# Between gathers: an add that nobody reads in place of a wait for a landing

## The chip, the core and the metric

One NeuronCore of one Trainium2 chip runs the kernel. The metric is the device time of one execution in microseconds. TensorE, VectorE, ScalarE, GpSimd and SyncE each run a list of instructions in order and meet through semaphores.

## The reference, cut to what matters

A graph layer over 3125 nodes with 256 features: `xn` is the layer norm of `x`, and

```
x = x + gnn(xn, src, dst, edge_weight) + mix(xn)      # mix: linear attention, then a small MLP
x = x + ffn(layernorm(x))                             # ffn: two of eight experts, chosen by a router

msgs = edge_val[:, None] * X[edge_col]                # gnn, 53125 edges
h = segment_sum(msgs, edge_row, num_segments=3125)
return h @ W.T + b
```

The kernel computes `X @ W.T` first (the tensor `xg_rows` in DRAM) and sums the weighted rows of it afterwards. The change is in the fetching of those rows.

## The kernel before, in words

**The columns.** The edges are sorted on the chip by destination tile of 128 nodes into 440 columns of 128 edges (`COLS`). For each column GpSimd issues one indirect DMA (`gather`, L705) that fetches the 128 source rows of 256 f32 from `xg_rows` into one of the 18 slots of `RING`, a part of the tile `ARENA`. VectorE makes a 128x128 selection matrix for it (`select`, L1277). TensorE multiplies the two (L1799), two columns at a time: a pair. VectorE adds each product to its tile of `X` (`add`, L1289). Six columns are a hand, and TensorE waits at the start of a hand until all its six gathers have landed. Three hands are a round of the ring. A gather into a slot that was used before waits until TensorE has finished the pair that read it (`chunk_mm`).

**Order of the work.** The first 132 columns (`COLS_A`) are worked off while the edges of the later groups are still being sorted; there GpSimd has a multiply (`group_columns`, L693) after every sixth gather. From column 132 on GpSimd only gathers; the first of these 308 gathers starts at 318.06 us and the last at 786.42. Beside these 308 columns the attention and the MLP run. In part A (12 steps, `a_transpose`, `a_project` L1850 and L1857, `a_outer` L1865) keys, values and queries are projected, and VectorE adds KS (L1338) and QT (L1341). In part B (12 full steps of seven pairs, `b_attend` L1895, `b_transpose` L1636, `b_hidden` L1913, `b_project` L1924) the attention output goes through VectorE and ScalarE (which writes XS, L900) and back to TensorE. The pairs are woven by hand between the steps: `pairs(p, p + 2)`, a piece of the step, and so on, and VectorE's `columns` in the same way. Every engine keeps this order, so what waits in it holds back all behind it.

**The wait that the change touches.** `BREATH` is 8. Before columns 132, 140, ... 436 (39 times) GpSimd waits until the gather issued last has landed: `landed(c - 1)` gives the semaphore of its hand and the count it then has.

**After the gathers** come the residuals, and the expert FFN from about 800 us on. SyncE loads the eight experts' first weights, 512 KB each, during the gathers, one for every nine pairs of even number (L591).

`Chain` counts the marks of one engine on one semaphore: `mark` adds one when the instruction is done, `settle` waits until all marks so far are in.

Of the kernel before, what the change touches and what calls it, by code (L numbers as in the profile page):

```python
# [5 lines left out]
def gps_layer_program(nc, x, row, col, weight, gnn_wT, gnn_b, qkv_wT, ln1_g, ln1_b, mix_w1T, mix_b1,  # L6
# [10 lines left out]
    ALU, ACT, AX = mybir.AluOpType, mybir.ActivationFunctionType, mybir.AxisListType  # L17

    P = 128
    N, C = out.shape  # L20
# [22 lines left out]
    HAND = 6  # L43
    HANDS = 3
    RC = HANDS * HAND
# [25 lines left out]
    with ctx:  # L71
        def sb(name, shape, dt=f32):
            return scope.enter_context(nc.sbuf_tensor(name, shape, dt))

        def sem(name):
            return ctx.enter_context(nc.semaphore(name))
# [11 lines left out]
        ROWC = sb("ROWC", [P, 5, C])  # L88
        B2R, L2G, L2B, FG, FB = (ROWC[:, n, :] for n in range(5))
        carrier = sb("carrier", [P, 1])  # L90
        eps_ln = sb("eps_ln", [P, 1])
        warm = sb("warm", [P, 1])
        ident = sb("ident", [P, P])
# [232 lines left out]
        gathered = [sem(f"gathered{h}") for h in range(HANDS)]  # L326
# [184 lines left out]
        def pair_bank(pair):  # L511
            return bank[(2 if pair < PAIRS_A else 6) + pair % 2]

        def landed(c):

            r, at = divmod(c, RC)
            return gathered[at // HAND], 16 * (r * HAND + at % HAND + 1)

        def per_chunk(m, G, n):

            return m[:, G * GC:(G + 1) * GC].rearrange("p (k o) -> p k o", o=1).to_broadcast([P, GC, n])
# [91 lines left out]
        def _(pool):  # L613
            chain = Chain(pool, pool_step)
# [83 lines left out]
            def gather(c):  # L698

                r, at = divmod(c, RC)  # L700
                k = at % HAND
                if r and k % 2 == 0:
                    pair = (c - RC) // 2
                    pool.wait_ge(chunk_mm[pair % 2], pair // 2 + 1)
                pool.indirect_dma_start(RING[:, at, :], None, xg_dram,  # L705
                                        bass.IndirectOffsetOnAxis(ap=SIX[:, c:c + 1], axis=0)
                                        ).then_inc(gathered[at // HAND], 16)
# [17 lines left out]
            pool.wait_ge(slots_ready, 2)  # L725
            for c in range(COLS_A, COLS):
                if (c - COLS_A) % BREATH == 0:
                    pool.wait_ge(*landed(c - 1))
                gather(c)


# [272 lines left out]
        def _(dve):  # L1004
# [260 lines left out]
            def targets(r, cols=RC):  # L1265

                _, base = nc.values_load_multi_w_load_instructions(
                    BID[0:1, bass.ds(r, 1), 0:cols].rearrange("p a c -> p (a c)"), engines=[mybir.EngineType.DVE],
                    min_val=0, max_val=(TILES - 1) * C,
                    skip_runtime_bounds_check_because="BID counts the buckets whose first column is at or before the "  # L1270
                    "column, less one: the first bucket starts at column 0, so it lies in 0 .. TILES - 1, times C")
                return base
# [235 lines left out]
            def over_sum(dst, width, n):  # L1508
# [14 lines left out]
            dve.wait_ge(topi_ready, 1)  # L1523
            dve.wait_ge(up_in, 16 * (NE + 1))
            _, chosen = nc.values_load_multi_w_load_instructions(
                RI[0:1, 0:TOPK], engines=[mybir.EngineType.DVE], min_val=0, max_val=NE - 1,
                skip_runtime_bounds_check_because="RI holds places of the NE experts that max_index found")
# [586 lines left out]
```

## Time and profile before

| | |
|---|---|
| median of 3 runs | 972.7 us (970.0 to 973.05) |
| the profiled execution | 975.65 us |
| its span | 973.9 us |
| TensorE busy (matmul) | 785.4 us, 81% |
| VectorE busy | 677.2 us, 70% |
| GpSimd busy | 584.6 us, 60% |
| ScalarE busy | 415.0 us, 43% |
| gathers, GpSimd's part | 440, 426.6 us, mean 0.97 us |

The span runs from the first to the last instruction; the execution's own time has 1.75 us around it. Busy time is the time inside instructions. "Idle before" is how long the engine had stood still when an instruction began, and the releaser is what ended it, as inferred from semaphores; "issue" means that the profile shows no releaser. The busy time of a gather is the time in which GpSimd writes its transfer list; the transfer itself goes on after it.

### The profile page before, as it was taken

What the parts mean: (1) busy time and instruction counts of PE and PEld (TensorE: products, weight loads), DVE (VectorE), ACT (ScalarE), POOL (GpSimd) and SP (SyncE); (2) the same over time, 40 slices, a digit from 0 to 9 for tenths busy, and PEclk for the clock granted to TensorE, in tenths of its full rate; (3) what the DMA queues carried; (4) which work ended last, traced back from release to release, by engine and by line L of the source; (5) the groups of instructions that cost most, each with busy time, mean ns of one, the idle gap of its engine ahead of it and who ended that gap; (6) DMA issues with size and microseconds to landing.
All of it is one profiled execution on the core that took longest, in us unless ns stands there. A gap on an engine that the chain in (4) does not pass through costs nothing.

```text
span 973.9 us, 14063 instructions
## 1 busy us (share of the span) xinstructions
PE 785.4 (81%) x4353; PEld 639.0 (66%) x4353; DVE 677.2 (70%) x1936; ACT 415.0 (43%) x1008; POOL 584.6 (60%) x648
## 2 busy tenths in 40 slices
PE   7879857887787888878777877777776677999997
PEld 5649846776676566546545655565555454999997
DVE  8989737999875546445545767677667567766776
ACT  2738724775772133313313222332223216666551
POOL 3847675878877666666666666666666610333353
PEclk9989977999989799999988988989989889999999
DMA  7210032333233433333233333333332521000000
GB/s 238 87 49 1 28 92 60 93 88 88 87 91 92 111 87 103 87 87 108 82 105 90 114 87 84 106 91 108 90 111 87 100 30 55 13 22 24 23 29 30
DMA packets 38994, 76.88 MB, mean 79 GB/s; under 512 B 9811, under 2 KB 22536, under 8 KB 38920
## 3 DMA queue, kind: packets, MB, share of 16 engines
q0 software_dynamic: 21120, 57.70, 21.5%
q1 hardware_dynamic: 17800, 18.29, 5.9%
q8 instruction: 35, 0.57, 0.2%
q14 instruction: 39, 0.32, 0.1%
HBM read 69.48 MB, written 6.48 MB: 78 GB/s over the span
## 4 chain that ended last, share of the span: by engine, by line
PE 33%; issue 14%; POOL 11%; DVE 9%; ACT 4%; another core or an unknown queue 2%; DMA 1%; DVEq 1%; POOLq 0%; ACTq 0%
PE bank L2008 14%; POOL ARENA L705 11%; PE bank L1799 7%; DVE X L1289 4%; PE bank L1850 4%; ACT OIA L824 2%; PE bank L1857 2%; PE bank L1865 1%; PE bank L1636 1%; PE bank L1757 1%; PE bank L1913 1%; DMA ARENA<-xg_rows,ARENA 1%; DVE ARENA L1277 1%; DVE ST L1029 1%
## 5 line engine op out<-in xcount | busy, mean ns | idle before, releaser
L705 POOL DMA_INDIRECT ARENA<-xg_rows,ARENA x440 | 426.6, 970 | 214.5 <-issue 118.0
L1289 DVE TENSOR_TENSOR X<-bank,X 128x256 f32 x440 | 185.0, 420 | 217.0 <-PE bank L1799 91.2
L1799 PE MATMUL bank<-ARENA 128*128 128x256 f32 x880 | 246.7, 421 | 97.1 <-DVE X L1289 53.2
L1799 PEld LDWEIGHTS bank<-ARENA 128*128 128x128 f32 x880 | 173.1, 208 | 148.4 <-DVE X L1289 67.0
L1277 DVE TENSOR_SCALAR ARENA<-iota,ARENA 128x128 f32<-128x128 f32 x440 | 153.4, 354 | 0.0
L1757 PE MATMUL bank<-OIA,ASA 128*128 128x128 f32 x676 | 95.3, 308 | 14.8 <-DVE ASA L1207 5.8
L1757 PEld LDWEIGHTS bank<-OIA,ASA 128*128 128x128 f32 x676 | 93.7, 224 | 18.5 <-issue 17.4
L824 ACT ACTIVATE OIA<-iota,LANE 128x128 f32<-128x128 f32 x286 | 86.0, 388 | 13.9 <-PE bank L1757 13.6
L992 ACT ACTIVATE HF<-bank,FB 128x262 f32<-128x262 f32 (+1 forms) x96 | 46.8, 488 | 42.0 <-PE bank L2008 22.5
L868 ACT ACTIVATE NK<-bank 128x256 f32<-128x256 f32 x25 | 9.7, 388 | 123.0 <-PE bank L1850 101.7
L2008 PE MATMUL bank<-QH,W1L 128*128 128x262 f32 (+1 forms) x192 | 55.9, 291 | 2.3 <-DVE W1L L1535 1.7
L2008 PE MATMUL bank<-QH,W1H 128*128 128x262 f32 (+1 forms) x192 | 55.2, 287 | 0.0
L2008 PE MATMUL bank<-QL,W1H 128*128 128x262 f32 (+1 forms) x192 | 55.1, 287 | 0.0
L693 POOL TENSOR_TENSOR ASA<-LHA,EPC 128x832 f32<-128x832 f32 x26 | 41.3, 1590 | 22.6 <-DVE LHA L1192 20.8
L2008 PE MATMUL bank<-W2H,HFL 128*128 128x256 f32 x192 | 54.0, 281 | 0.0
L2008 PE MATMUL bank<-W2H,HFH 128*128 128x256 f32 x192 | 54.0, 281 | 0.0
L2008 PE MATMUL bank<-W2L,HFH 128*128 128x256 f32 x192 | 53.9, 281 | 0.0
L1850 PE MATMUL bank<-QKVW,XT 128*128 128x512 f32 x100 | 49.3, 639 | 0.0
L734 POOL TENSOR_TENSOR XN<-XN,B2C 128x256 f32<-128x256 f32 x25 | 18.8, 752 | 47.7 <-DVE B2C L1566 47.7
L992 ACT ACTIVATE HFH<-bank,FB 128x262 fp32r<-128x262 f32 (+1 forms) x96 | 47.0, 490 | 0.0
L833 ACT COPY GSW<-bank 64x128 f32<-64x128 f32 x32 | 8.3, 258 | 82.7 <-remote 32.4
L1574 DVE TENSOR_TENSOR HFL<-HF,HFH 128x262 fp32r<-128x262 f32 (+1 forms) x96 | 40.1, 467 | 4.2 <-ACT HFH L992 3.9
(317 smaller groups left out, 1532.6 us busy)
## 6 DMA issues: line engine op xcount, KB each, us to landing
ARENA<-xg_rows,ARENA POOLq DMA_INDIRECT x440
FW1A<-in_exp_w SPq DMA_DIRECT2D x8, 512.0 KB
xg_rows<-XGS SPq DMA_DIRECT2D x12, 256.0 KB, 2.1
out<-YO SPq DMA_DIRECT2D x24, 128.0 KB, 1.7
X<-in_x SPq DMA_DIRECT2D x1, 1664.0 KB, 12.7
X<-in_x SPq DMA_DIRECT2D x1, 1536.0 KB, 8.3
FW<-in_exp_w SPq DMA_DIRECT2D x2, 512.0 KB, 4.4
QKVW<-in_qkv_wT SPq DMA_DIRECT2D x1, 768.0 KB
```

Of the source, the lines that this page charges most:

```text
L693: made = pool.tensor_tensor(into[:, :, LC:2 * LC], lh, per_chunk(EPC, G, LC), ALU.mult)
L705: pool.indirect_dma_start(RING[:, at, :], None, xg_dram, bass.IndirectOffsetOnAxis(ap=SIX[:, c:c + 1], axis=0)).then_inc(gathered[at // HA ...
L824: ins = act.activation(into[:, k, :], iota[:, :], ACT.Abs, scale=-1.0, bias=LANE[:, G * GC + k:G * GC + k + 1])
L992: ins = act.activation(into, bank[s][:, 0:width], ACT.Gelu, bias=FB1[:, n // FJ, n % FJ:n % FJ + 1])
L1277: ins = V.tensor_scalar(SEL[:, t % 2 * HAND + k, :], iota[:, :], SLO[:, at], SW[:, at], ALU.is_equal, ALU.mult)
L1289: V.tensor_tensor(xt, pair_bank(pair)[:, half * C:(half + 1) * C], xt, ALU.add).then_inc(x_added, 1)
L1574: V.tensor_tensor(HFL[par][:, n, 0:width], HF[:, s, 0:width], HFH[par][:, n, 0:width].bitcast(f32), ALU.subtract).then_inc(hl_ready, 1)
L1757: ins = T.matmul(bank[s][:, 0:P], left[:, k, :], right[:, k, :], start=(k == 0), stop=(k == GC - 1))
L1799: ins = T.matmul(pair_bank(pair)[:, u * C:(u + 1) * C], SEL[:, t % 2 * HAND + k, :], RING[:, h * HAND + k, :], start=True, stop=True)
L1850: ins = T.matmul(bank[2 + s][:, :], XT[:, c, s, :], QKVW[:, c, C:3 * C], start=(c == 0), stop=(c == CC - 1))
L1857: ins = T.matmul(bank[5][:, h * 2 * P:h * 2 * P + n], QKVW[:, c, h * P:(h + 1) * P], XT[:, c, 0:len(slots), :], start=(c == 0), stop=(c == ...
L2008: ins = T.matmul(into, left, right, start=(m == 0), stop=(m == len(terms) - 1))
```

## The change

In place of the wait for a landing, GpSimd waits for its own last mark (`settle`) and adds the rows L2G and FG (128x256 each) into `rest`, a new tile that nothing reads. The count of gathers, their order, the ring and every other wait stay. `landed` goes, since nothing calls it.

```diff
         carrier = sb("carrier", [P, 1])
+        rest = sb("rest", [P, C])
...
-        def landed(c):
-
-            r, at = divmod(c, RC)
-            return gathered[at // HAND], 16 * (r * HAND + at % HAND + 1)
...
             for c in range(COLS_A, COLS):
                 if (c - COLS_A) % BREATH == 0:
-                    pool.wait_ge(*landed(c - 1))
+                    chain.settle()
+                    chain.mark(pool.tensor_tensor(rest[:, :], L2G, FG, ALU.add))
                 gather(c)
```

## Rows read from the trace of the kernel before

**Rows 1.** The page: shares of the chain of work that ended last, by engine.

```profile
PE 33%; issue 14%; POOL 11%; DVE 9%; ACT 4%; another core or an unknown queue 2%; DMA 1%; DVEq 1%; POOLq 0%; ACTq 0%
```

**Rows 2.** Waits of TensorE, 330 to 570 us: total us, times, longest.

```profile
PE bank L1799 <- issue: 12.8, 6, 4.2
...
PE bank L1799 <- DMA ARENA<-xg_rows,ARENA: 0.5, 1, 0.5
```

**Rows 3.** The same, 570 to 790 us.

```profile
PE bank L1799 <- issue: 20.7, 11, 5.3
...
PE bank L1799 <- DMA ARENA<-xg_rows,ARENA: 3.5, 2, 2.2
```

**Rows 4.** Timeline, GpSimd and TensorE: start, us, instruction, idle before.

```profile
689.90 0.95 POOL L705 DMA_INDIRECT ARENA<-xg_rows,ARENA  x1 [0.30 <-issue]
...
692.72 1.10 PE L1799 MATMUL bank<-ARENA 128*128 128x256 f32 x4 [3.43 <-issue]
```

**Rows 5.** Timeline of GpSimd around a multiply between gathers.

```profile
210.13 0.95 POOL L705 DMA_INDIRECT ARENA<-xg_rows,ARENA  x1 [0.30 <-issue]
211.10 1.59 POOL L693 TENSOR_TENSOR ASA<-LHA,EPC 128x832 f32<-128x832 f32 x1
212.85 0.99 POOL L705 DMA_INDIRECT ARENA<-xg_rows,ARENA  x1 [0.16 <-PE bank L1799]
```

**Rows 6.** Timeline of GpSimd: gathers before and behind waits for a landing.

```profile
329.82 0.95 POOL L705 DMA_INDIRECT ARENA<-xg_rows,ARENA  x1 [2.04 <-DMA ARENA<-xg_rows,ARENA]
...
338.60 0.95 POOL L705 DMA_INDIRECT ARENA<-xg_rows,ARENA  x1 [0.30 <-issue]
341.62 0.95 POOL L705 DMA_INDIRECT ARENA<-xg_rows,ARENA  x1 [2.07 <-DMA ARENA<-xg_rows,ARENA]
...
514.90 0.94 POOL L705 DMA_INDIRECT ARENA<-xg_rows,ARENA  x1 [2.13 <-DMA ARENA<-xg_rows,ARENA]
...
766.59 0.95 POOL L705 DMA_INDIRECT ARENA<-xg_rows,ARENA  x1 [2.12 <-PE bank L1799]
```

**Rows 7.** The chain in order of time: start, us; L1850 in A, L1913 in B.

```profile
335.54 3.85 PE bank L1850 x8
...
375.51 3.43 PE bank L1850 x8
...
388.14 3.43 PE bank L1850 x8
...
510.53 1.73 PE bank L1850 x4
...
528.73 3.78 PE bank L1913 x8
...
755.67 1.73 PE bank L1913 x8
```

**Rows 8.** Waits of TensorE, 534 to 650 us, first half of B.

```profile
PE bank L1636 <- ACT XS L900: 11.1, 4, 3.8
...
PE bank L1799 <- issue: 1.5, 1, 1.5
```

**Rows 9.** Timeline of TensorE and GpSimd near the last gathers.

```profile
776.07 2.05 PE L1799 MATMUL bank<-ARENA 128*128 128x256 f32 x4 [5.34 <-issue]
...
787.61 6.67 PE L1799 MATMUL bank<-ARENA 128*128 128x256 f32 x16 [3.91 <-issue]
...
782.49 0.94 POOL L705 DMA_INDIRECT ARENA<-xg_rows,ARENA  x1 [6.20 <-DMA ARENA<-xg_rows,ARENA]
```

**Rows 10.** Groups of GpSimd: busy us, mean ns, idle before.

```profile
L735 POOL TENSOR_TENSOR X<-X,ROWC 128x256 f32<-128x256 f32 x25 | 21.3, 851 | 0.0
L734 POOL TENSOR_TENSOR XN<-XN,B2C 128x256 f32<-128x256 f32 x25 | 18.8, 752 | 47.7 <-DVE B2C L1566 47.7
```

**Rows 11.** Timeline: a gather beside VectorE's QT addition.

```profile
384.80 1.82 POOL L705 DMA_INDIRECT ARENA<-xg_rows,ARENA  x1 [0.30 <-issue]
...
385.11 0.69 DVE L1341 TENSOR_TENSOR QT<-QR,EQ 128x512 f32<-128x512 f32 x1
```

## The prediction

> **What bounds the kernel now.** I first read the chain of work that ended last [rows 1]. TensorE's own work is a third of it, GpSimd 11%, and "issue" 14%, which is time in which an engine stood still and the profile names no releaser. The change touches only the last 308 of the 440 gathers (columns 132 to 439), which run from about 318 to 787 us, so the question is what TensorE stands still for there. The waits of TensorE over that stretch say it [rows 2, 3]: its pair matmuls (L1799) were idle before 12.8 us by "issue" and 0.5 by a named gather in 330 to 570 us, and 20.7 and 3.5 in 570 to 790 us. One case in the timeline shows what "issue" is [rows 4]: the sixth gather of a hand starts at 689.90 and ends at 690.85, and the pair that needs it starts at 692.72, 1.87 us after, having idled 3.43 us. So a gather lands some 1.9 us after GpSimd has finished it, and TensorE stood waiting for that landing. The four entries add up to 37.5 us. That is the most that quicker gathers can give while TensorE's other waits stay as they are.
>
> Then GpSimd itself. Inside a run of gathers one starts every 1.25 us (0.95 of work, 0.30 of gap). Every eighth time the wait for the landing makes the gap 2.07 us instead of 0.30: the gather at 338.60 and the next at 341.62 [rows 6]. Eight gathers and a breath took (514.90 - 329.82) / 15 = 12.34 us in the attention's first part and (766.59 - 514.90) / 21 = 11.99 us after it [rows 6], so 1.54 and 1.50 us a column.
>
> **The change, part by part.**
>
> *The wait that goes.* There are 39 of them (132, 140, ... 436). Each costs 2.07 - 0.30 = 1.77 us of GpSimd's time.
>
> *The add that comes.* 39 adds of 128x256 f32, two inputs in SBUF. This very form stands in the trace: 25 at a mean of 0.75 us (L734) and 25 at 0.85 (L735) [rows 10]. What an add costs between gathers is seen where GpSimd multiplies between two of them [rows 5]: the multiply of 1.59 us starts as soon as the gather ends, and the gathers on either side start at 210.13 and 212.85, 2.72 us apart where 1.25 is usual. So the insertion costs 1.47 us, its own 1.59 less 0.12, and the gather behind it is 0.04 longer. For an add of 0.75 to 0.85 this is 0.67 to 0.77; between gathers I take 0.68, since the 0.85 comes from a stretch where VectorE too works on SBUF operands most of the time. The settle in front of it asks for the add of eight gathers before, which is long done, so it costs nothing; what hides the add's own completion is 10 us of gathers, and without that cover it would cost at most the add's length again.
>
> *Net on GpSimd.* 1.77 - 0.68 = 1.09 us a time, 42.5 us in all. A breath then takes 12.34 - 1.09 = 11.25 us in the first part, 1.41 a column, and 10.90 later, 1.36 a column.
>
> *What TensorE makes of it, first part (A).* A step of the attention's first half holds on average 4.83 pairs, 9.67 columns (by the source, pairs 66 to 123 over 12 steps). By the chain, twelve steps took 510.53 - 335.54 = 175.0 us, 14.58 each; a step in which TensorE had columns enough took 388.14 - 375.51 = 12.63 [rows 7]. The new gather rate allows 9.67 x 1.41 = 13.6 us a step, and GpSimd, which starts A with a lead, may spend it. I take 13.5: 12 x 1.1 = 13 us. Bounds: 6 us if the waits on VectorE's KS and sums take half of it back, 19 us if steps of 13.0 are reached.
>
> *Second part (B).* Eleven steps of 7 pairs, 14 columns, took (755.67 - 528.73) / 11 = 20.63 us [rows 7]. The new gather rate allows 14 x 1.36 = 19.1, which would be 17 us. But here I doubt it. In 534 to 650 us TensorE hardly waited for gathers (1.5 us), and was no quicker; it stood 11.1 us for ScalarE's XS in the transposes [rows 8]. These waits are those of B's own loop (attend, VectorE's sums, ScalarE's scaling, transpose), and where gathers are late they hide behind them. So B may give nothing (its own loop is as slow as the gathers) or 17. I take 8, half way, as the rows show both kinds of step.
>
> *The end.* At 770 to 788 us gathers land very late once: GpSimd waits 6.20 us for one, and TensorE 5.34 and 3.91 us [rows 9]. A GpSimd that is not halted after every eighth gather runs ahead until the ring of 18 stops it, so it would have several columns in hand there. I take 6 of the 9.25 us; bounds 0 and 9.25.
>
> *VectorE.* The add reads SBUF, as do VectorE's KS and QT additions. Beside QT (385.11, 0.69 us) a gather took 1.82 us instead of 0.95 [rows 11]: the two do get in each other's way. The Trainium skill (SBUF — State Buffer, Who interferes with whom) says that a VectorE instruction with two SBUF inputs and a GpSimd instruction that reads SBUF exclude each other for a whole instruction, whoever starts first. It speaks against the change: if each add blocked VectorE once for its length it would be 39 x 0.75 = 29 us of VectorE. The common VectorE instruction here, L1289, has one input in PSUM, and by the source the two-input ones are five or so in a step. If one add in ten meets one it is 4 x 0.75 = 3 us, most of it beside VectorE's own idle time; I put it at nothing and leave 3 us for the range. Nothing else is moved: SyncE's weight loads hang on the pair counter and come earlier with it.
>
> Sum: 13 + 8 + 6 = 27 us. The profiled execution took 975.65 us (span 973.9 and 1.75 around it), so 948.6. The median of the runs is 2.95 lower; if the late landings at the end belong to this execution alone, the gain is smaller and the start lower as well. By the median it would be 945.7; I say 947.
>
> **The rivals.**
>
> 1. *TensorE's and VectorE's own loops are the bound nearly throughout* (gain 6 to 15 us, 960 to 970). For it: B's first half, where no gather was waited for and the steps were as long [rows 7, 8]. Against it: A's quick steps of 12.63 and the 37.5 us of waits for landings. Worked out: A's lower bound 6, B 0, the end 0, is 970; with A's 13 it is 963.
>
> 2. *All of the waiting for gathers goes* (37.5 us, 938). For it: the new rate in B, 19.1 us a step, is well below what the steps take, and lateness at the start of a hand spreads to VectorE. Against it: XS waits.
>
> 3. *Slower: the halt kept the gathers in a good state.* Without it more transfers may be in flight, and landings like that at 782 us (6.20 instead of 2.07) become common. One such episode costs TensorE 5.34 + 3.91 = 9.25 us [rows 9]. Against 27 us gained, three more cancel the gain; from the fourth on the kernel is slower, with six 975.65 - 27 + 55 = 1004. Against it: halting every eighth time did not prevent that one, and the gathers before 318 us run without any such wait, six and a multiply in 5 x 1.25 + 2.72 = 9.0 us (1.5 a column, the mean rate of the later ones too), at 0.95 each [rows 5]. What the trace cannot show is more than the 14 in a row that the source issues at its start.
>
> 4. *The swap does nothing*: an add between gathers costs as much as the halt, 1.77 us, because engine changes are dear. [Rows 5] exclude it nearly: no gap before the multiply, 0.16 behind it.
>
> **How the numbers follow.** Forecast, 940 to 960: 0.52. Rival 2 (below 940): 0.12. Rival 1 (960 to 970): 0.20. Rivals 4 and a total absorption, within 0.3% (2.9 us, about what a measurement of this kernel can tell from no change): 0.08. Rival 3: 0.08. Range 935 to 969: it leaves out some 2 in 10, and takes in the bounds (13 + 8 + 6 becomes 6 + 0 + 0 or, capped, 37.5, and 3 us more for the slightly quicker matmuls of an engine that stands less, as the eight of L1850 took 3.85 us in one step and 3.43 in another [rows 7]). Faster 0.84, same 0.08, slower 0.08.
>
> **What would show it right or wrong.** In the changed kernel's timeline of GpSimd: after every eighth gather an add of 0.75 us with no gap, then 0.16, and no "DMA" releaser; from gather 132 on some gaps released by TensorE's pairs, the sign that the ring is full. The last gather should start 30 us or more earlier than 786.42. TensorE's waits on "issue" and gathers at L1799 should fall from 37.5 us to under 15, A's steps to 13.5, B's to 19.9. If B's steps stay at 20.6 with the XS waits grown, rival 1 holds. If gathers take longer than 0.95 us in bulk, or landings longer than 1.9, rival 3. I would be wrong above all if the lead of the gathers is eaten by VectorE, which is busy 70% of the span and works its column sums in order with everything else.

## The result: slower, and what the profile after shows

The changed kernel takes 981.2 us (median of 7 runs, 977.0 to 986.0), the kernel before 973.1 on the same chip (7 runs, 970.0 to 976.4). The ratio is 1.0092, with a 95% interval of 1.0062 to 1.0121. It is slower by 0.9%, where 2.7% faster was forecast. The profiled execution took 977.0 us (span 975.3), the quickest of its runs; that of before took 975.65, one of the slower of its. So the two traces show why the gain of 27 us is not there, and only 1.4 of the 8 us of loss.

**GpSimd did what was forecast around the adds.** Its timeline around a new add, then its waits from 318 to 800 us (total us, times, longest). They answer to [rows 5, 6]:

```profile
338.58 0.95 POOL L701 DMA_INDIRECT ARENA<-xg_rows,ARENA  x1 [0.30 <-issue]
339.54 0.74 POOL L725 TENSOR_TENSOR rest<-ROWC 128x256 f32<-128x256 f32 x1
340.44 0.97 POOL L701 DMA_INDIRECT ARENA<-xg_rows,ARENA  x1 [0.16 <-issue]
```

```profile
POOL ARENA L701 <- issue: 79.6, 277, 0.3
POOL ARENA L701 <- remote: 29.0, 19, 3.0
POOL ARENA L701 <- PE bank L1796: 23.9, 12, 5.8
```

The add follows the gather at once, the next gather 0.16 us behind it, and no DMA releases anything. Apart from one wait of 3.4 us at the first add, GpSimd halts only where the ring is full: 12 times on a pair of TensorE and 19 times on "remote". So the last gather starts only 6.6 us earlier, at 779.83 instead of 786.42, where 30 us or more were forecast: the ring gave most of the lead back.

**TensorE no longer waits for gathers.** Its waits before pairs, 318 to 800 us:

```profile
PE bank L1796 <- DVE X L1286: 31.4, 21, 4.4
...
PE bank L1796 <- issue: 2.3, 4, 1.2
```

The 37.5 us of [rows 2, 3] (37.7 over this whole stretch) have become 2.3, and no gather is named.

**Something else grew.** In the chain of work that ended last, GpSimd's 11% of [rows 1] are gone. VectorE has doubled, and "another core or an unknown queue" went from 2 to 7%:

```profile
PE 31%; DVE 18%; issue 11%; another core or an unknown queue 7%; ACT 3%; DVEq 1%; POOLq 0%; POOL 0%; ACTq 0%
```

There is no other core here. The label means that a semaphore rose at a time at which no recorded instruction ended. In the lists of waits the same thing is called "remote". VectorE's waits before its column adds, 318 to 800 us, first before the change, then after:

```profile
DVE X L1289 <- PE bank L1799: 80.4, 40, 6.9
DVE X L1289 <- issue: 56.8, 28, 7.0
DVE X L1289 <- remote: 37.5, 20, 4.3
```

```profile
DVE X L1286 <- remote: 73.5, 27, 8.3
DVE X L1286 <- PE bank L1796: 62.8, 33, 7.4
DVE X L1286 <- issue: 25.3, 22, 4.8
```

One episode shows what is behind it. The timelines of the changed kernel's engines, 338 to 355 us:

```profile
342.99 1.10 PE L1796 MATMUL bank<-ARENA 128*128 128x256 f32 x4 [1.56 <-DVE X L1286]
354.25 2.13 PE L1862 MATMUL bank<-VX,KS 128*128 128x132 f32 x8 [10.16 <-DVE KS L1335]
...
350.51 0.42 DVE L1286 TENSOR_TENSOR X<-bank,X 128x256 f32 x1 [7.41 <-remote]
...
353.09 1.11 DVE L1335 TENSOR_TENSOR KS<-KR,EXK 128x512 f32<-128x512 f32 x1
...
345.98 0.38 ACT L865 ACTIVATE NK<-bank 128x256 f32<-128x256 f32 x1 [11.36 <-remote]
...
346.72 0.95 POOL L701 DMA_INDIRECT ARENA<-xg_rows,ARENA  x1 [0.30 <-issue]
350.65 0.94 POOL L701 DMA_INDIRECT ARENA<-xg_rows,ARENA  x1 [2.98 <-remote]
```

TensorE's last pair is recorded from 342.99 to 344.09, and its projections (L1847) as ended by 338.40. ScalarE, which reads them, could go on at 345.98 and 350.20. VectorE, which reads the pairs, stood for 7.41 us until 350.51, and TensorE then stood for 10.16 us for VectorE's KS. Even GpSimd, whose ring was full, stood 2.98 us. The trace also holds the times at which semaphores rose. I set each rise of a TensorE semaphore beside the recorded end of the matmul that raises it:

```
semaphore of        matmul ended   semaphore rose
a pair   (L1796)    333.82         336.76
a pair   (L1796)    334.96         341.71
project  (L1847)    336.68         345.96
project  (L1847)    338.40         350.18
         (L1854)    340.12         350.27
         (L1633)    340.56         350.33
a pair   (L1796)    341.43         350.39
a pair   (L1796)    344.09         350.45
```

The last five come 0.06 to 0.09 us apart, up to 11.8 us after their work. The burst comes 3.5 us after the last gather started, when GpSimd had stood idle since 347.67. I call this a held update. The ends of matmuls are modelled, so "late" has some slack, but the starts are recorded and the next matmuls had begun. The engines that read the results did start only behind the late rises. Whether the rise alone is late, or the writing of the result before it, the trace does not tell.

I then counted the held updates, in 318 to 790 us: rises over 1 us after the end of the instruction that causes them, among those for which the trace has both.

```
          TensorE: late / recorded, sum    VectorE late    ScalarE late
before    55 / 230, 125 us                 0 of 366        0 of 90
after     77 / 221, 262 us                 0 of 372        0 of 92
```

Before had them too. In 800 to 974 us, where GpSimd gathers nothing, none of some 150 is over 0.3 us late in either kernel. The first 113 us, ahead of the first gather, show the same: none of 95 before and of 92 after is late. Between 113 and 318 us, where the first 132 gathers run with a multiply after every sixth, 37 to 45 of some 105 are late in every kernel of this document (before 44 of 102, 137 us in all; after 41 of 110, 120 us).

By the starts of TensorE's pairs, 66 to 124, to 208, to 219: the first part (A) went from 176.7 to 181.5 us, the second (B) from 248.6 to 255.6, the end from 35.6 to 25.0. That is 4.8 + 7.0 - 10.6 = 1.2 us, near the difference of the two profiled spans (1.4). The first step of A alone, with the episode above, went from 14.95 to 24.42 us.

**The two parts lost their time in different ways.** The same stretches, with the busy time of PE, PEld, DVE, ACT and POOL, the granted clock, the DMA share and GB/s; first A and B before the change, then A and B after:

```profile
331.92:508.65 176.73, 145.01 (x568) 99.63 (x568) 87.32 (x259) 54.65 (x134) 115.91 (x116) 0.94 0.33 95
508.65:757.23 248.58, 186.98 (x820) 144.49 (x819) 173.92 (x645) 72.86 (x123) 157.78 (x166) 0.92 0.33 96
```

```profile
331.75:513.27 181.52, 141.89 (x568) 100.21 (x567) 89.65 (x260) 55.18 (x134) 133.06 (x137) 0.92 0.33 97
513.27:768.80 255.53, 198.34 (x820) 153.87 (x819) 180.94 (x648) 72.87 (x123) 177.22 (x191) 0.87 0.33 95
```

In A, TensorE stands longer, 39.6 us instead of 31.7. The waits for gathers fell from 13.3 to 1.9 us, but those for KS rose from 9.4 to 18.4 and those of pairs for VectorE's adds from 2.9 to 11.3. VectorE's "remote" in this stretch rose from 8.6 to 44.6 us: all of its growth is here. In B, "remote" did not grow (28.9 us before, 26.1 after), and TensorE stands 4.4 us *less*, 57.2 instead of 61.6. There the same 820 matmuls are busy for 198.3 us instead of 187.0, with a granted clock of 0.87 instead of 0.92: it was at 1.2 GHz, the lower of its two levels, for 68 of 256 us where it had been for 41 of 249. This is not of the profiled execution alone: the seven runs of the change were granted 0.901 to 0.917 over the whole of them (mean 0.910), the kernel before 0.921 in the mean of its 64 runs beside the experiments, on four chips. In the episode above the clock was at 1.2 GHz from 344.5 to 358.2 us, through TensorE's stand and 4 us beyond it. Whether the held updates are what lowers it in B no run isolates; the last table has it for every kernel.

### The profile page after: what moved, and what is told of

Its sections match the earlier page's. It is cut to its first block, busy times and chain, and to the rows that moved or that the text cites. A ratio compares the mean times of both kernels' runs of the same rounds, so it can differ in the third digit from the quotient of the medians.

```text
span 975.3 us, 14064 instructions
## 1 busy us (share of the span) xinstructions
PE 792.4 (81%) x4353; PEld 646.4 (66%) x4353; DVE 682.0 (70%) x1936; ACT 415.3 (43%) x1008; POOL 613.5 (63%) x687
## 4 chain that ended last, share of the span: by engine, by line
PE 31%; DVE 18%; issue 11%; another core or an unknown queue 7%; ACT 3%; DVEq 1%; POOLq 0%; POOL 0%; ACTq 0%
PE bank L2005 14%; DVE X L1286 8%; PE bank L1796 6%; PE bank L1847 2%; DVE ARENA L1274 2%; PE bank L1633 1%; PE bank L1862 1%; PE bank L1754 1%; PE bank L1854 1%; PE bank L1921 1%; DVE ST L1026 1%; DVE KS L1335 1%; DVEq L1264 1%; DVE TX L1380 1%
## 5 line engine op out<-in xcount | busy, mean ns | idle before, releaser
L1796 PE MATMUL bank<-ARENA 128*128 128x256 f32 x880 | 242.8, 417 | 65.5 <-DVE X L1286 61.4
L1274 DVE TENSOR_SCALAR ARENA<-iota,ARENA 128x128 f32<-128x128 f32 x440 | 157.9, 364 | 0.0
L889 ACT ACTIVATE SD<-MV,eps_ln 128x2 f32<-128x2 f32 (+1 forms) x26 | 6.5, 289 | 93.3 <-DVE MV L1368 75.5
L1847 PE MATMUL bank<-QKVW,XT 128*128 128x512 f32 x100 | 45.0, 592 | 0.0
```

The lines of the kernel that those rows point to most:

```text
L1274: ins = V.tensor_scalar(SEL[:, t % 2 * HAND + k, :], iota[:, :], SLO[:, at], SW[:, at], ALU.is_equal, ALU.mult)
L1796: ins = T.matmul(pair_bank(pair)[:, u * C:(u + 1) * C], SEL[:, t % 2 * HAND + k, :], RING[:, h * HAND + k, :], start=True, stop=True)
L1847: ins = T.matmul(bank[2 + s][:, :], XT[:, c, s, :], QKVW[:, c, C:3 * C], start=(c == 0), stop=(c == CC - 1))
```

## The experiments

The main theory: GpSimd's back-to-back gathers hold TensorE's semaphore updates, the halt of 1.77 us let them out, and the add of 0.74 does so less. The time is then a sum of two terms that the breaks trade: TensorE starved by a slow GpSimd, and its readers starved by held updates. The expectations call this H or T. They leave out the granted clock, which turned out to be a third term. Rivals are named with the runs. The ratios are to the kernel before on the same chip. At the end of this section a table has all runs.

### No wait and no add

```diff
             for c in range(COLS_A, COLS):
-                if (c - COLS_A) % BREATH == 0:
-                    chain.settle()
-                    chain.mark(pool.tensor_tensor(rest[:, :], L2G, FG, ALU.add))
                 gather(c)
```

> The changed kernel without its add: after the 132nd gather nothing stands between gathers but the ring. Theory H (TensorE's semaphore updates are held back while gathers are in flight and let go when none is): gathers are in flight more of the time than with the add, so no faster than the changed kernel, 979 to 990 us, and late updates as many as there. Rival V (the add itself costs, in VectorE's SBUF operands): the cost goes with the add, 973 us or less. Rival L (the loops of TensorE and VectorE are the bound, gathers or not): 973 to 981, with no more late updates than before.

Measured: 995.0 us, ratio 1.0243 [1.0206, 1.0279]. With the least for GpSimd to do the kernel is the slowest so far, 14 us above the change. So the add's own work is not what costs: taking the 39 adds away makes it worse. Of my figures for this run even the highest was too low. The sign is that of the theory, but the amount is not explained by it: the held updates are 62, 232 us in all, fewer than with the add (77, 262 us). From pair 66 to pair 219 TensorE stands 7 us longer than in the changed kernel, and is busy 10 us longer with the same matmuls at a lower clock (0.872 instead of 0.890).

### Two adds, three adds

```diff
                 if (c - COLS_A) % BREATH == 0:
-                    chain.settle()
-                    chain.mark(pool.tensor_tensor(rest[:, :], L2G, FG, ALU.add))
+                    for _ in range(2):        # e3: range(3)
+                        chain.settle()
+                        chain.mark(pool.tensor_tensor(rest[:, :], L2G, FG, ALU.add))
                 gather(c)
```

> Two adds in place of the wait: the gathers' run is broken for about 1.6 us, which is less than the 1.9 us that a gather takes to land after GpSimd is done with it. H: the flight is never quite empty, so late updates stay as in the changed kernel; 976 to 985 us. V: twice the adds, 985 to 992. L: 973 to 978.

> Three adds in place of the wait: a break of some 2.4 us, longer than the landing takes, with no wait on any gather. H: the updates are let go at every break as in the kernel before, so late ones fall to its level, and the time falls below that of two adds although GpSimd does more: 971 to 979 us. V: three times the adds, 995 or more. L: like two adds or slower by GpSimd's longer breaks, 978 to 990.

Two adds: 972.6 us, ratio 0.9976 [0.9950, 1.0002]. Three: 988.2 us, ratio 1.0135 [1.0114, 1.0157]. The theory's figures missed both times, and both ways: 976 to 985 and 971 to 979 us. Of what it said of the updates it had more right: with two adds as many are late as in the changed kernel (79, 214 us), with three fewer than before the change (41, 84 us). Waits before pairs and before column adds, 318 to 800 us, with two adds, then three:

```profile
PE bank L1797 <- issue: 9.5, 7, 4.5
...
DVE X L1287 <- remote: 46.8, 21, 6.9
```

```profile
PE bank L1797 <- issue: 41.6, 23, 5.8
...
PE bank L1797 <- DMA ARENA<-xg_rows,ARENA: 11.3, 5, 3.8
...
DVE X L1287 <- remote: 13.2, 6, 4.0
```

With no, one, two and three adds the times are 995, 981, 973 and 988: more useless work made the kernel quicker twice and then slower. The two terms are seen to trade: VectorE's "remote" falls from 73.5 (one add) to 46.8 and 13.2 us, TensorE's waiting for gathers grows from 2.3 to 9.5 and 52.9. My figure for three adds was too low, since I had left out what the longer break costs GpSimd. From gather to gather over a break it is 3.46 us at the median with three adds, 2.69 with two and 3.04 with the old halt. The third add is thus 0.8 us, some 30 us over 39 breaks, and the break is longer than the halt that the change removed. The chain of the run with three adds has GpSimd in it again, with a fifth:

```profile
PE 27%; POOL 21%; issue 12%; DVE 8%; ACT 2%; another core or an unknown queue 2%; DVEq 1%; DMA 0%; POOLq 0%
```

### No gathers beside the attention

From column 132 on an add into the ring slot takes the place of each gather (the sums hold no messages from there on), with semaphores of its own for TensorE's wait.

```diff
+                if c < COLS_A:
                     pool.indirect_dma_start(...).then_inc(gathered[at // HAND], 16)
+                else:
+                    pool.tensor_tensor(RING[:, at, :], L2G, FG, ALU.add).then_inc(filled[at // HAND], 1)
...
             for c in range(COLS_A, COLS):
-                if (c - COLS_A) % BREATH == 0:
-                    pool.wait_ge(*landed(c - 1))
                 gather(c)
```

> From column 132 on each gather is left out and GpSimd adds two rows into the ring's slot in its place (the sums then lack the messages of these columns); TensorE waits for these adds instead. The same matrix work, order and ring, but no gather in flight. H: no late updates of TensorE after the last gather, steps of part A at 12.6 us all, of part B well under 20; 895 to 930 us. L: part B's steps remain at 20 us since its own loop sets them: 955 to 970. V: 308 adds instead of 39, 975 or slower.

Measured: 935.5 us, ratio 0.9604 [0.9584, 0.9624], 5.5 us above my range (895 to 930) and 20 us below the rival's (955 to 970). VectorE's waits, then TensorE's:

```profile
DVE X L1291 <- PE bank L1805: 85.4, 42, 6.3
DVE X L1291 <- issue: 13.0, 12, 1.8
```

```profile
PE bank L1638 <- ACT XS L902: 29.6, 13, 3.1
PE bank L1871 <- DVE KS L1340: 23.5, 12, 2.7
...
PE bank L1805 <- issue: 3.1, 1, 3.1
```

"Remote" has gone, and 1 of 303 recorded updates is late. GpSimd has no halt but the ring's, as in the first experiment, and 308 adds in SBUF where that has none. The engines' own loops would let this kernel end at 935.5. So they do not bound it (rival 1), and what costs 60 us in the first experiment comes with the gathers: TensorE from pair 66 to pair 219 stands 71 us instead of 109 and is busy 350 us instead of 370.

### Transfers by SyncE, no gathers by GpSimd

As above, and behind each of the eight weight loads SyncE loads 18 times 128 KB from `xg_rows` into a tile that nothing reads.

```diff
+                for n in range(18):
+                    sp.dma_start(spare[:, :], xg_dram[n * P:(n + 1) * P, :]).then_inc(spare_in, 16)
+                    sp.wait_ge(spare_in, 16 * (18 * e + n + 1))
```

> The kernel without gathers after column 132 (935.5 us), and SyncE loads 128 KB eighteen times behind each of the eight weight loads into a tile that nothing reads, each waited for, so that plain loads of a gather's size are in flight much of the time. If any transfer in flight holds TensorE's updates: VectorE's waits for held updates return (20 us or more) and the time is 945 or more. If only gathers made by GpSimd do: none of such waits, 933 to 940.

Measured: 941.2 us in a single run, 1.2 us above the upper figure that I had if only GpSimd's gathers hold updates, and below the 945 of any transfer. The traffic is there, in the view of DMA issues for 318 to 520 us, in loads of the size of a gather:

```profile
spare<-xg_rows SPq DMA_DIRECT2D x49, 128.0 KB, 2.0
```

VectorE has no "remote", and of 300 recorded updates none is late. Bytes in flight do not hold an update when SyncE issues the loads. They were 43 and 60 GB/s in the two halves against 94 before, so this is not the gathers' full traffic. Nor does it tell what it is about GpSimd's gathers: in no run does GpSimd issue plain loads, or another engine gathers.

### Gathers of 32 rows

The kernel with neither wait nor add, but each gather from column 132 on fetches 32 rows instead of 128 (the sums lack three quarters of the messages).

```diff
+                few = P if c < COLS_A else P // 4
-                pool.indirect_dma_start(RING[:, at, :], None, xg_dram,
-                                        bass.IndirectOffsetOnAxis(ap=SIX[:, c:c + 1], axis=0)
+                pool.indirect_dma_start(RING[0:few, at, :], None, xg_dram,
+                                        bass.IndirectOffsetOnAxis(ap=SIX[0:few, c:c + 1], axis=0)
```

> The kernel with nothing between gathers, but each gather after the 132nd fetches 32 rows instead of 128 (a quarter of the bytes and of the list; the sums lack three quarters of these messages). If what holds the updates is the amount in flight or the landing: few held updates, VectorE's waits for them under 20 us, 940 to 960 us. If it is a gather's fixed work, whatever its size: held as with full gathers, 55 us or more, 985 to 1000.

Measured: 1021.5 us, ratio 1.0481 [1.0445, 1.0518]. My ranges were 940 to 960 if the amount in flight holds the updates and 985 to 1000 if a gather's fixed work does; the time is above both. A quarter of the bytes (30 GB/s in 318 to 520 us, where whole gathers moved 96), and the slowest kernel of all. Two gathers of it, and VectorE's waits:

```profile
403.52 0.86 POOL L702 DMA_INDIRECT ARENA<-xg_rows,ARENA  x1 [0.30 <-issue]
404.69 0.87 POOL L702 DMA_INDIRECT ARENA<-xg_rows,ARENA  x1 [0.30 <-issue]
```

```profile
DVE X L1284 <- PE bank L1794: 105.8, 43, 5.7
DVE X L1284 <- remote: 77.7, 21, 7.9
```

GpSimd's part of a gather hardly shrinks with the rows (0.86 instead of 0.95 us), and gathers start every 1.17 instead of 1.25 us. About as many updates are held as with whole gathers (60, 201 us, against 62 and 232). So they do not hang on the bytes. They do not explain either why this kernel is 26 us slower than the one with whole gathers: from pair 66 to pair 219 TensorE stands as long in both (109 us), and is busy 384 us instead of 370, at a clock of 0.844 instead of 0.872. Another 9 us had been lost by pair 66.

### Other halts: every 6, 12 and 16, and a shorter one

The kernel before with `BREATH` 6, 12 or 16, and then with a wait once a hand for the gather before the last, which was to halt 0.65 us instead of 1.77 (measured, 0.50 at the median):

```diff
-        BREATH = 8
+        BREATH = 6          # e7: 12, e8: 16
```

```diff
-                if (c - COLS_A) % BREATH == 0:
-                    pool.wait_ge(*landed(c - 1))
+                if c % HAND == 1:
+                    pool.wait_ge(*landed(c - 2))
```

> The kernel before with a wait for the landing at every sixth gather instead of every eighth. H: fewer held updates than before (VectorE's waits for them under 30 us), but GpSimd pays 1.77 us a time for 52 halts instead of 39, 23 us more, and it is the bound already: 988 to 998 us. P: the same sign, since it too gets more free time; 985 to 998.

> A wait for the landing at every twelfth gather. GpSimd saves 13 halts, 23 us, so that TensorE's 37 us of waiting for gathers fall to under 10. H: updates are held through twelve gathers instead of eight and VectorE's waits for them rise from 37 us to 55 or so; the two about cancel: 965 to 980 us. P: the free time falls by a third, 975 to 985.

> A wait for the landing at every sixteenth gather. Starving gone, as with twelve; H: held updates between those of twelve and those of the kernel with nothing between its gathers: 975 to 990 us. P: 985 to 995.

> The kernel before, but the wait stands two gathers behind the end of each hand of six and asks for the gather before the last one: GpSimd halts about 0.65 us every six gathers, and one gather is always in flight. Theory H (TensorE's updates are held until no gather is in flight), with its price now the sum of two terms, waiting for gathers and held updates: no starving, updates held as in the kernel with nothing between its gathers, 985 to 998 us, and VectorE's waits for held updates 55 us or more. Rival P (only the share of time without a gather being issued counts, not an empty flight): this break is as much time per gather as two thirds of one add, so about 981.

Measured: 994.0 us at every sixth (1.0187 [1.0139, 1.0235]), 1000.6 at every twelfth (1.0244 [1.0190, 1.0298]), 997.2 at every sixteenth (1.0237 [1.0159, 1.0316]); the shorter halt 980.9 (1.0062 [1.0030, 1.0095]). Rows of the runs with 6 and with 12, 318 to 800 us:

```profile
PE bank L1799 <- issue: 54.0, 22, 5.8
...
DVE X L1289 <- remote: 7.8, 4, 2.2
```

```profile
PE bank L1799 <- issue: 3.0, 3, 2.3
...
DVE X L1289 <- remote: 97.2, 25, 11.2
```

Of the four distances eight is the best, and the two sides lose in different ways: at 6 TensorE starves, at 12 and 16 VectorE stands for held updates and the granted clock is lower (0.903 over the runs, where 6 has 0.921). The run with 6 was forecast right. That with 12 was 21 us above the top of my range and that with 16 was 7 us above it, since I took the loss to grow slowly with the distance of the breaks. The shorter halt had its 55 us of "remote" and more (79.4), but refuted the time that I had from the length of one break (985 to 998), and met that of the rival, by which the share of GpSimd's time without gathers counts (981).

### Where the breaks are

One add every fourth column (`BREATH = 4` in the changed kernel), and two adds up to column 263 with the old wait from there on:

```diff
+                    if c < 264:
+                        for _ in range(2):
+                            chain.settle()
+                            chain.mark(pool.tensor_tensor(rest[:, :], L2G, FG, ALU.add))
+                    else:
+                        pool.wait_ge(*landed(c - 1))
```

> The changed kernel with its add at every fourth gather instead of every eighth: the same 78 adds as with two at every eighth, but in breaks of 0.9 us instead of 1.75. If the length of a break counts (TensorE's updates come out in breaks of 1.7 us and more): held as in the changed kernel or worse, 978 to 990 us. If only GpSimd's free share counts: as with two adds at every eighth, 970 to 975 us.

> Two adds in place of the wait up to column 263 (part A), the wait for the landing from column 264 on (part B). Theory T (two terms: TensorE waits for gathers, and its semaphore updates are held while gathers follow each other; a break's length and place trade them): A as with two adds, 4 us shorter than before, B as before but entered with a lead of gathers, so that the late landings at the end are covered: 963 to 972 us. Rival N (two adds' 972.6 is chance within what differs from run to run): 972 to 978.

Measured: 974.7 us (1.0025 [0.9994, 1.0056]) and 976.7 us (1.0020 [0.9992, 1.0047]), neither to be told from before. Twice as many short breaks do nearly what half as many of double length do (974.7 and 972.6 us). That speaks for the share of free time. For the mix the theory had 963 to 972 us, and the rival, by which the 972.6 us of two adds is chance, 972 to 978: the rival was right. The mix is no better than either of its halves.

### All runs

"Starved" is TensorE's wait before pairs on "issue" and on gathers, "remote" VectorE's before column adds, both in 318 to 800 us; "held" is the sum of late updates, counted as above, with their number. "Stood" and "busy" are TensorE's from pair 66 to pair 219, "clock" the granted clock of that stretch, all of the profiled execution.

```
                          us      ratio    starved  remote   held        stood   busy   clock
no gathers                935.5   0.9604     3.1      0        3 (1)      71.3   349.5  0.929
the same, SyncE loads     941.2   -          0        0        0 (0)      75.4   347.6  0.935
two adds every 8          972.6   0.9976     9.5     46.8    214 (79)     92.8   362.1  0.900
before: wait every 8      973.1   1         37.7     37.5    125 (55)    106.2   354.8  0.915
one add every 4           974.7   1.0025     5.8     56.7    171 (61)     94.8   364.6  0.880
two adds, later waits     976.7   1.0020     1.3     78.2    210 (73)     98.9   367.2  0.875
short wait every 6        980.9   1.0062     6.8     79.4    290 (83)     93.3   367.8  0.876
after: one add every 8    981.2   1.0092     2.3     73.5    262 (77)    102.1   360.0  0.890
three adds every 8        988.2   1.0135    52.9     13.2     84 (41)    113.4   359.8  0.909
wait every 6              994.0   1.0187    63.5      7.8     24 (14)    116.2   363.1  0.903
nothing                   995.0   1.0243     3.8     60.1    232 (62)    109.1   369.7  0.872
wait every 16             997.2   1.0237     7.1     65.6    231 (67)    109.6   369.3  0.872
wait every 12            1000.6   1.0244     3.0     97.2    239 (65)    118.9   370.2  0.876
nothing, 32 rows         1021.5   1.0481     5.5     77.7    201 (60)    108.6   384.4  0.844
```

Of the versions that fetch all their messages none beats the kernel before: the interval of two adds touches 1. Of those that gather, the kernel before is the least busy with its matmuls; it is others, such as two adds, that stand less.

## Why the prediction was wrong

**What was right.** *The wait that goes* and *The add that comes*: an add of 0.76 us on average (39 in 29.6 us), the gather 0.16 us behind it, and GpSimd ahead until the ring stopped it. That excludes rival 4. *The end* was right and undersized: 10.6 us came back where I took 6 and had 9.25 as the bound. The starving fell further than forecast, to 2.3 us where I said under 15. On *VectorE*: the KS additions took 9.6 us for 13 instead of 8.6. Two of them overlapped an add of GpSimd and took 1.11 us (at 353.09, above) and 1.20 where the others took 0.68; so the adds blocked VectorE for about 1 us in all, within the 3 us that I had left. The Trainium skill (SBUF — State Buffer, Who interferes with whom) says that a VectorE instruction with two SBUF inputs contends with a GpSimd instruction that reads SBUF, and these two additions agree. But the run without adds, slower by 14 us than the change, shows that it is not where the time went.

**The step that failed** is *What TensorE makes of it*, for both parts. I priced them by the gather rate alone (13.6 us a step in A, 19.1 in B) and took 13 and 8 us of gain; measured by pair starts they lost 4.8 and 7.0 (15.1 and 21.3 us a step). The sentence that failed with it is the cap, that 37.5 us could be gained "while TensorE's other waits stay as they are". They did not stay. From pair 66 to pair 219 the waits for gathers all but vanished, and TensorE stood 102.1 us instead of 106.2: all but 4 us were taken back by its waits for VectorE and ScalarE. In A this is the work of held updates, as VectorE's "remote" (8.6 to 44.6 us) and the stand of 10.16 us for KS show. The halt had a second effect, which I put at nothing: it let TensorE's semaphore updates out. For B I had let quicker matmuls of a TensorE that stands less widen the range by 3 us. They came out 11.4 us slower in all at the lower granted clock (0.87 instead of 0.92), and this, not standing, is B's loss; why the clock fell there stays open. The late landing of [rows 9] is another matter: there the gather itself landed at 782.2 us, and TensorE's updates of that stretch are on time. It did not come back in the changed kernel.

**The profile of before had it.** The 2% of "another core or an unknown queue" in [rows 1] stood for a releaser that a kernel on one core cannot have, and VectorE's list of waits, which I did not bring into the sum, had 37.5 us of "remote" beside 37.7 us of starving. I read only the one list, TensorE's. The growth of "remote" is also no measure of the loss by itself: VectorE's waits before column adds fell in all, since those on "issue" went from 56.8 to 25.3 us and those on pairs from 80.4 to 62.8. It says what VectorE stood for, and not how much more. And the smooth run of GpSimd's first 132 gathers, which I held against rival 3, was smooth for GpSimd alone: 44 of TensorE's 102 recorded updates of that stretch are late.

**The rivals.** Rival 3 named the sign and the place (the halt keeps something in a good state) at a chance of 0.08, but with the wrong mechanism: landings. In the changed kernel gathers take 0.97 us, as before, and TensorE waits for none. The run without gathers refutes rival 1. Rival 2's premise came true, since nearly all of the waiting for gathers went, but not its time. My last sentence, that VectorE might eat the lead, named the engine. But it was standing, not busy: its column adds have 137.0 us of work in 318 to 800 us where they had 136.3.

**Shown, and open.** Shown: the held updates go with GpSimd's gathers (14 to 83 late ones in each of the twelve kernels that gather, 1 and 0 in the two that don't, and 37 to 45 beside the first 132 columns in all fourteen), not with GpSimd being busy, not with bytes moved, not with the adds. Shown too: in the runs with 12 and 16 columns between halts the time is longer while TensorE starves less, and the episode of A shows a held update stopping VectorE and then TensorE.

Not shown: that the held updates are the whole of the loss. Neither "remote" nor "held" orders the kernels: with nothing between gathers they are 60.1 and 232 us at 995 us, with one add 73.5 and 262 at 981. ScalarE waits for late updates as well (11.36 us in the episode), and it matters which one is held: the step of A with the episode alone took 9.5 us more. The granted clock is the other part. It is highest in the two kernels without held updates (0.929 and 0.935) and next in the three with the fewest (0.915, 0.909 and 0.903 at 125, 84 and 24 us); the others have 0.844 to 0.900. That fits a clock that falls with what held updates do to TensorE, but no run changes the one without the other. And part B by itself speaks against a simple rule: there the kernel without gathers was granted 0.886, less than the 0.918 of the kernel before. The two profiled executions differ by 1.4 us, so 7 of the 8 us between the medians are in neither trace. Whether the length of a break or the share of GpSimd's time in them decides is open as well; two runs favour the share. Why a gather's issue holds an update of TensorE, and hardly any of VectorE or ScalarE, no run here tells.

## What to carry to other kernels

A wait that looks useless in one engine's list can be what keeps another engine's signals moving. So before it goes, read the waits of all engines, above all those whose releaser is "remote" or "unknown" in a kernel on one core, and cap the gain by what they may take back. After the change, compare not only how long TensorE stands but also how long the same matmuls take and the clock they were granted: here one part of the kernel lost by the first and the other by the second. Where GpSimd issues gathers back to back beside TensorE's work, the spacing of the gathers is a setting to be measured in both directions: here 6 and 12 columns between halts were each about 2% slower than 8. When a removed stall moves the time little or the wrong way, one run with the suspect work taken out altogether (here the gathers) shows at once whether the price belongs to the loops or to the suspect.

## What was unexpected in the hardware

- While GpSimd issued indirect DMAs every 1.25 us, rises of TensorE's semaphores came up to 11.8 us after the recorded end of the matmul; none of VectorE's 372 and ScalarE's 92 in the changed kernel was over 1 us late, and in the other kernels one of VectorE's at most. With adds in place of the gathers 1 of 303 of TensorE's was, and with SyncE's 128 KB loads beside them 0 of 300.
- Held updates come out in bursts some 0.06 us apart, often when GpSimd has started no gather for 2 to 3 us: in the kernel before some 70% of those over 0.3 us late (53 of 75) came more than 1.9 us after the last start, at a median of 2.7 us. In the changed kernel it was 51 of 91, and most of the others came within 1.3 us of a start. In the kernel before, those beyond 1.9 us lay 0.03 us after the last landing at the median; in the run with 32 rows they lay 0.8 us after it, and 3.0 after the start. Neither distance is the same in all kernels, so what lets them out is open.
- A gather of 32 rows costs GpSimd 0.86 us, one of 128 rows 0.95.
- In 113 to 318 us, with a multiply of GpSimd after every sixth gather, TensorE's updates are late as well (44 of 102, up to 9.6 us, in the kernel before); ahead of the first gather none of 95 is.
- With the same matmuls, TensorE's busy time from pair 66 to pair 219 ran from 347.6 us (granted clock 0.935) to 384.4 (0.844) over the kernels.
- It is self-limiting: when the ring is full, GpSimd waits for a TensorE update that is itself held (19 waits on "remote" in the changed kernel, at most 3.0 us), and in the episode above its standing still was followed by the updates.
